# Causal attention: a head's ten transpositions in one row, the third chunk through another PSUM bank

## The chip, the cores and the metric

The kernel runs on one core of a Trainium2 chip. The metric is the device time of one execution in microseconds (us). The core's engines run side by side, each through its own list of instructions in order: TensorE (PE in the rows, its weight loads PEld), VectorE (DVE), ScalarE (ACT), GpSimd (POOL), and SyncE (SP), which issues most transfers. They wait for each other through semaphores. TensorE writes to PSUM, which has eight banks of 128x512 fp32 here; DVE and ACT read it.

## The reference

Two transformer layers on x of shape (4, 512, 512), fp32. The change lies in the attention of the first layer: 32 query heads and 8 key and value heads of width 128, causal, with rotary position codes.

```
q = (x @ wq).reshape(B, T, H, HD).transpose(0, 2, 1, 3)        # k and v alike, with 8 heads
q = q * cos + _rotate_half(q) * sin                             # k alike
scores = jnp.einsum('bhtd,bhsd->bhts', q, k) * (1.0 / np.sqrt(HD))
scores = jnp.where(mask, scores, -jnp.inf)
att = jax.nn.softmax(scores, axis=-1)
out = jnp.einsum('bhts,bhsd->bhtd', att, v)
return out.transpose(0, 2, 1, 3).reshape(B, T, H * HD) @ wo
```

The rest of the reference (layer norms with modulation, a sign-weight layer, a second attention over the heads of each position, a layer of routed low-rank experts) lies in other stages, which the change does not touch.

## The kernel before

The batch is worked in two halves of two items. In each half the attention of the first layer is one stage, `stage_groups`, which goes through 64 heads (32 query heads times two items). Every product is made of three products in a faster format: each operand is split into a high part, rounded by a cast on ACT (or DVE), and a low part, the difference, formed on DVE (or POOL). So a 128x512 result of one projection takes 4 x 3 = 12 products on TensorE.

The engines' lists are written out by hand in one loop over n, the head. At step n TensorE does the following (`block.tensor`, from line 788): it waits until head n's probabilities are normalised, transposes them (`turn`, line 698), projects a key or a value where one is due, forms the scores of head n+1, projects the query of head n+2, and then works on the pair p = n // 2: at an odd n it weighs the values (`weigh_early`, `weigh_late`), at an even n it multiplies three of the four output tiles of the pair before with the output weights (`out_proj`; the fourth comes at the odd n). A key is due at n = 5, 9, 13, ..., 57 (and at the very start), a value at n = 2, 6, ..., 58; the later text calls the former key steps and the latter value steps. At n = 4, 8, 12, ... and at n = 3, 7, 11, ... neither is due.

A head's probabilities under the causal mask are ten 128x128 blocks. They are transposed in three chunks of 4, 3 and 3 blocks (`PT_CHUNK`). Chunk 0 goes to bank pT0, chunk 1 to pT1, chunk 2 to pT0 again. ACT casts each chunk into `pth` (`pt_his`, line 865), then DVE subtracts into `ptl` (`pt_los`, line 978). Before, chunks 0 and 1 stand at the start of the step. Chunk 2 stands after the scores of head n+1 at a key step, ahead of the query's projection, and after the query's projection at all others:

```
turn(n, ((0, (0,)), (1, (1,))))
for e in step_e(n, 1): project(e)          # key or value
if n + 1 < NH: scores(n + 1)
if key_step(n): turn(n, ((2, (2, 3)),))
for e in step_e(n, 0): project(e)          # query
if not key_step(n): turn(n, ((2, (2, 3)),))
```

ACT and DVE have chunk 2 at the matching places of their lists. A projection lies in bank pj, and the next one may not begin before the last has been taken out: ACT writes two rotated half copies (lines 843 and 844), DVE multiplies by the cosine (`leave`, line 945), POOL multiplies by the sine and adds (lines 1143 and 1146), DVE casts the query's high part (line 963), POOL forms the low part (line 1155). For a head's softmax, DVE takes the maxima while it copies out of PSUM (`maxes`, line 974), ACT exponentiates (line 860), DVE takes the reciprocal and scales four rows of blocks (`norms`, lines 994 and 998).

The output tiles of `out_proj` go into bank pW, the second of each four into bank pO; `weigh_early` writes pO too. DVE adds each tile to the sum in SBUF (`add`, line 1006). So the third tile of a pair waits in pW for the addition of the first. At an even step DVE's list ends with the cosine of the query, the split of chunk 2, at value steps the split of the value, the addition of the first tile, the query's cast, the additions of the second and the third tile. In the first half, from n = 56 on, `modulate` puts other products between the second and the third tile.

Of the kernel before, what the change touches and what calls it, by code (L numbers as in the profile page):

```python
# [14 lines left out]
F32 = mybir.dt.float32  # L15
# [487 lines left out]
def stage_groups(nc, held, a, wts, half):  # L503
# [4 lines left out]
    with Stage(nc, f"gqa{half}") as st:  # L508
# [19 lines left out]
        pT = [st.ps(f"pT{i}", [P, T]) for i in range(2)]  # L528
        pO, pW = st.ps("pO", [P, T]), st.ps("pW", [P, D])
        early, late = (p[:].rearrange("p (h t) -> p h t", h=2) for p in (pO, pS[2]))  # L530
        qkv_in, wo_in = st.sem("qkv_in"), st.sem("wo_in")
# [41 lines left out]
        def last_split(kinds, group):  # L573
            return max(n for n, s in enumerate(SPLIT_LIST) if s[0] in kinds and s[2] == group) + 1

        def key_step(n):

            return any(PROJ[e][0] == "K" for e in step_e(n, 1))

# [4 lines left out]
        with nc.Block() as block:  # L584
# [39 lines left out]
            def _(pe):  # L624
# [74 lines left out]
                def turn(n, jobs):  # L699
                    for k, js in jobs:  # L700
                        if k == 0 and later and n > LATER_AT + 1:
                            pe.wait_ge(chunk_left, n - LATER_AT - 1)
                        if 3 * n + k >= 2:

                            pe.wait_ge(pt_lo, (3 * n, 3 * n - 1, 3 * n + 1)[k])
                        if k == 1 and n % R0 == R0 - 1 and n + 1 < NH:
                            pe.wait_ge(v_lo, n // R0 + 2)
                        if k == 1 and n == 0:
                            pe.wait_ge(v_lo, 1)
                        for j in js:  # L710
                            for i in range(j, TT):
                                c = PT_OFF[j] - PT_CHUNK[k][0] + (i - j) * P
                                mm = pe.transpose(pT[k % 2][:, c:c + P],  # L713
                                                  prob[n % 2][:, P_OFF[i] + j * P:P_OFF[i] + (j + 1) * P], held.ident)
                        mm.then_inc(pt_full, 1)
# [12 lines left out]
                def weigh_early(p):  # L728

                    if p == 0:  # L730
                        pe.wait_ge(cosed, 2)
                    else:
                        pe.wait_ge(w_added, TT * (p - 1) + 2)
                    pe.wait_ge(v_lo, 2 * p // R0 + 1)
                    weigh(p, early, [(0, 0, 0, PT_OFF[0], 2 * P), (1, 1, P, PT_OFF[1], P)])
# [7 lines left out]
                def out_proj(d):  # L743
# [4 lines left out]
                    if i == 0:  # L748
                        pe.wait_ge(o_lo, 2 * pair + 2)
                        pe.wait_ge(w_lo, split_no("o", (2 * pair + 1) % R0, pair // (R0 * HB // 2)))  # L750
                    before = [f for f in range(max(0, d - TT), d) if wbank(f) is wbank(d)]
                    if before:
# [37 lines left out]
                for n in range(NH):  # L790
# [3 lines left out]
                    pe.wait_ge(normed, n + 1)  # L794
                    turn(n, ((0, (0,)), (1, (1,))))
                    for e in step_e(n, 1):
                        project(e)
                    if n + 1 < NH:
                        scores(n + 1)
                    if key_step(n):  # L800
                        turn(n, ((2, (2, 3)),))
                    for e in step_e(n, 0):
                        project(e)
                    if not key_step(n):
                        turn(n, ((2, (2, 3)),))
                    if n % R0 == 2 and n // R0 + 1 < UNITS:
# [23 lines left out]
            def _(act):  # L830
# [33 lines left out]
                def pt_his(n, ks):  # L864
                    for k in ks:
# [3 lines left out]
                        c, w = PT_CHUNK[k]  # L869
                        nc.scalar.copy(pth[:, n % 2, c:c + w], pT[k % 2][:, 0:w]).then_inc(pt_hi, 1)  # L870

# [29 lines left out]
                for n in range(NH):  # L901
                    if n == 0:
                        for e in STEP_PROJ[0]:
                            leave(e)
                    pt_his(n, (0, 1))
                    for e in step_e(n, 1):
# [3 lines left out]
                    if n == NH - 2:  # L910
                        act.wait_ge(rope_lo, len(ROPE))
                        act.dma_start(x[:, TT:2 * TT, :], a["x"][(half * HB + 1) * T:(half * HB + 2) * T, :].rearrange("(j p) d -> p j d", p=P)
                                      ).then_inc(x_back, 16)
                    if key_step(n):
                        pt_his(n, (2,))
                    for e in step_e(n, 0):
                        leave(e)
                    if not key_step(n):
                        pt_his(n, (2,))
                    if n % R0 == 2 and n // R0 + 1 < UNITS:  # L920
# [15 lines left out]
            def _(dve):  # L936
# [41 lines left out]
                def pt_los(n, ks):  # L978
                    for k in ks:
                        dve.wait_ge(pt_hi, 3 * n + k + 1)  # L980
                        c, w = PT_CHUNK[k]
                        nc.vector.tensor_tensor(ptl[:, n % 2, c:c + w], pT[k % 2][:, 0:w], pth[:, n % 2, c:c + w].bitcast(F32),  # L982
                                                ALU.subtract).then_inc(pt_lo, 1)
# [97 lines left out]
                for n in range(NH):  # L1081
                    if n == 0:
                        for e in STEP_PROJ[0]:
                            leave(e)
                    pt_los(n, (0, 1))
                    for e in step_e(n, 1):
# [9 lines left out]
                    if n == NH - 1:  # L1096
                        first_residual(2)
                    if key_step(n):
                        pt_los(n, (2,))
                    for e in step_e(n, 0):  # L1100
                        leave(e)
                    if not key_step(n):
                        pt_los(n, (2,))
                    if n == NH - 1:
# [956 lines left out]
```

## Time and profile before

| | us |
|---|---|
| median of 3 runs (lowest 2176.83, highest 2181.4) | 2180.11 |
| the profiled execution's own time | 2177.08 |
| its span, first to last instruction | 2175.1 |
| PE busy (11441 products) | 1987.6 |
| DVE busy | 1483.2 |
| ACT busy | 1067.9 |
| POOL busy | 1039.8 |

The mean granted clock of TensorE is 0.957 of full speed. Over the two long stretches of `stage_groups` (100 to 750 us and 1200 to 1850 us) it is 1.00, and there the rows repeat every four heads. A row's time is the start; two products of 512 columns start about 0.23 us apart though each is drawn 0.39 us long, since they are pipelined. So the intervals between starts tell TensorE's pace, and its busy share does not.

### The profile page before, as it was taken

To read this page: it belongs to the slowest core of one execution; us is meant where nothing else is said; L and a number is where in the kernel's file an instruction comes from. 1 tells how busy PE (TensorE), PEld (TensorE's weight loads), DVE (VectorE), ACT (ScalarE), POOL (GpSimd) and SP (SyncE) were. 2 spreads that over 40 slices of the span, in tenths; PEclk is the share of its full clock that TensorE was granted. 3 is DMA by queue.
4 is the path that set the end of the run, shared out by engine and by line. 5 is a ranking of instruction groups with operands and counts; after the bars stand their busy time and mean duration, and the time that the engine had idled before them with its cause. 6 is when DMAs were issued, how large, how long until landed. Compare 5 with 4: busy or idle time off the path is not lost. (4 is left out here: it accounts for less than half of the span.)

```text
span 2175.1 us, 33305 instructions
## 1 busy us (share of the span) xinstructions
PE 1987.6 (91%) x11441; PEld 1596.0 (73%) x11441; DVE 1483.2 (68%) x3679; ACT 1067.9 (49%) x2422; POOL 1039.8 (48%) x801
## 2 busy tenths in 40 slices
PE   4899999999999996897948999999999999978797
PEld 3788888888888774475527888888888888745664
DVE  4666676766767666966756767676676667779386
ACT  3555555555555552433235555555555555543232
POOL 3546564645646431544046555555555555417241
PEclk8999999999999997898969999999999999988899
DMA  5000101011010234146321101010110100041561
GB/s 171 20 30 20 30 20 30 20 30 49 20 30 20 78 107 139 64 101 129 85 95 41 30 12 38 20 30 20 30 49 8 42 20 1 30 141 39 116 123 39
DMA packets 132007, 115.30 MB, mean 53 GB/s; under 512 B 43201, under 2 KB 93441, under 8 KB 131841
## 3 DMA queue, kind: packets, MB, share of 16 engines
q1 hardware_dynamic: 124784, 105.51, 16.8%
q10 hardware_dynamic: 7056, 7.68, 1.2%
q8 instruction: 93, 1.52, 0.3%
q14 instruction: 74, 0.60, 0.1%
HBM read 92.15 MB, written 16.81 MB: 50 GB/s over the span
## 5 line engine op out<-in xcount | busy, mean ns | idle before, releaser
L860 ACT ACTIVATE gqa_prob<-gqa_prob,gqa_nmax 128x256 f32<-128x256 f32 (+3 forms) x512 | 284.2, 556 | 154.9 <-DVE gqa_nmax L974 146.6
L870 ACT CAST gqa_pth<-gqa_pT 128x384 fp32r<-128x384 f32 (+1 forms) x384 | 185.5, 519 | 205.3 <-PE gqa_pT L713 202.9
L974 DVE CUSTOM_DVE_ANT_0 gqa_prob<-gqa_pS,consts 128x256 f32<-128x256 f32 (+3 forms) x512 | 222.7, 486 | 58.9 <-PE gqa_pS L677 56.9
L1143 POOL TENSOR_TENSOR x<-x,consts 128x512 f32<-128x512 f32 x80 | 107.3, 1341 | 312.3 <-ACT x L844 312.3
L1143 POOL TENSOR_TENSOR y<-y,consts 128x512 f32<-128x512 f32 x80 | 107.3, 1342 | 303.1 <-ACT y L844 303.1
L982 DVE TENSOR_TENSOR gqa_ptl<-gqa_pT,gqa_pth 128x384 fp32r<-128x384 f32 (+1 forms) x384 | 217.2, 594 | 24.4 <-ACT gqa_pth L870 24.3
L713 PE MATMUL gqa_pT<-consts,gqa_prob 128*128 128x128 f32 x1280 | 183.8, 275 | 20.7 <-DVE gqa_ptl L982 19.2
L655 PE MATMUL gqa_pj<-first_hh,wqh 128*128 128x512 f32 x496 | 195.9, 395 | 0.0
L655 PE MATMUL gqa_pj<-first_hh,wql 128*128 128x512 f32 x496 | 194.7, 393 | 0.0
L655 PE MATMUL gqa_pj<-first_hl,wqh 128*128 128x512 f32 x496 | 194.1, 391 | 0.0
L713 PEld LDWEIGHTS gqa_pT<-consts,gqa_prob 128*128 128x128 f32 x1280 | 154.3, 141 | 48.8 <-DVE gqa_prob L998 15.1
L998 DVE TENSOR_SCALAR gqa_prob<-gqa_prob,gqa_rden 128x128 f32<-128x128 f32 (+3 forms) x512 | 186.4, 427 | 4.6
L758 PE MATMUL gqa_pW<-woh,gqa_oh 128*128 128x512 f32 x380 | 163.3, 430 | 9.7 <-DVE x L1006 5.3
L677 PE MATMUL gqa_pS<-gqa_kh,gqa_qh 128*128 128x256 f32 (+3 forms) x512 | 165.5, 334 | 0.0
L677 PE MATMUL gqa_pS<-gqa_kl,gqa_qh 128*128 128x256 f32 (+3 forms) x512 | 156.6, 324 | 0.0
L758 PE MATMUL gqa_pW<-wol,gqa_oh 128*128 128x512 f32 x380 | 151.0, 397 | 0.0
L758 PE MATMUL gqa_pW<-woh,gqa_ol 128*128 128x512 f32 x380 | 150.8, 397 | 0.0
L677 PE MATMUL gqa_pS<-gqa_kh,gqa_ql 128*128 128x256 f32 (+3 forms) x512 | 144.4, 323 | 1.3 <-POOL gqa_ql L1155 1.3
L655 PE MATMUL gqa_pj<-first_hh,wkvh 128*128 128x512 f32 x248 | 104.2, 420 | 22.3 <-PEq L83 22.3
L994 DVE RECIPROCAL gqa_rden<-gqa_den 128x4 f32<-128x4 f32 x128 | 22.8, 178 | 136.3 <-ACT gqa_prob L860 136.3
L877 ACT CAST gqa_oh<-gqa_pS 128x512 fp32r<-128x512 f32 x64 | 37.5, 586 | 147.3 <-PE gqa_pS L724 147.3
L655 PEld LDWEIGHTS gqa_pj<-first_hh,wqh 128*128 128x128 f32 x496 | 93.2, 188 | 20.6
(333 smaller groups left out, 5284.4 us busy)
## 6 DMA issues: line engine op xcount, KB each, us to landing
raw_o<-in_wo SPq DMA_DIRECT2D x16, 1024.0 KB, 5.2
raw_q<-in_wq SPq DMA_DIRECT2D x14, 1024.0 KB, 5.6
raw_q<-in_wmod SPq DMA_DIRECT2D x10, 1024.0 KB, 5.2
raw_kv<-in_wkv SPq DMA_DIRECT2D x14, 512.0 KB, 6.8
vp<-mid_hf SPq DMA_DIRECT2D x64, 64.0 KB, 1.8
kp<-mid_hf SPq DMA_DIRECT2D x16, 256.0 KB, 2.3
qp<-mid_hf SPq DMA_DIRECT2D x16, 256.0 KB, 2.5
tail_bd<-vp SPq DMA_DIRECT2D x64, 64.0 KB, 3.0
```

The lines of the kernel that those rows point to most:

```text
L655: mm = pe.matmul(bank[e][:], wp, hp[:, k, t], start=(n == 0), stop=(n == 3 * KT - 1))
L677: mm = pe.matmul(pS[s][:, c:c + wide], qp[r][:, t], kp[u % 2][:, 0:wide], start=(m == 0), stop=(m == 2))
L713: mm = pe.transpose(pT[k % 2][:, c:c + P], prob[n % 2][:, P_OFF[i] + j * P:P_OFF[i] + (j + 1) * P], held.ident)
L758: mm = pe.matmul(wbank(d)[:], op[pair % 2][:, h % 2, t], wp[:, h % R0, :], start=(m == 0), stop=(m == 5))
L860: ins = nc.scalar.activation(p, p, ACT.Exp, scale=-1.0, bias=nmax[r][:, i:i + 1], accum_out=den[r][:, i:i + 1])
L870: nc.scalar.copy(pth[:, n % 2, c:c + w], pT[k % 2][:, 0:w]).then_inc(pt_hi, 1)
L877: nc.scalar.copy(oh[p % 2][:, :, part * HALF_T:(part + 1) * HALF_T], (early, late)[part]).then_inc(o_hi, 1)
L974: nc.vector.tensor_tensor_reduce(prob[r][:, P_OFF[i]:P_OFF[i] + w], pS[s][:, c:c + w], held.mask[:, T - w:T], -1.0, LARGEST, ALU.add, ALU.min,
L982: nc.vector.tensor_tensor(ptl[:, n % 2, c:c + w], pT[k % 2][:, 0:w], pth[:, n % 2, c:c + w].bitcast(F32), ALU.subtract).then_inc(pt_lo, 1)
L994: nc.vector.reciprocal(rden[n % 2][:], den[n % 2][:]).then_inc(recip, 1)
L998: ins = nc.vector.tensor_scalar(p, p, rden[n % 2][:, i:i + 1], None, ALU.mult)
L1143: nc.gpsimd.tensor_tensor(rot[r % 2][:], rot[r % 2][:], held.sinT, ALU.mult).then_inc(sined, 1)
```

## The change

All three chunks of head n are now transposed in a row at the start of the step, on TensorE, ACT and DVE. Chunk 2 goes to bank pO in place of pT0. With that go new waits: chunk 2 waits until pO has been emptied, at an odd head by DVE's addition of the pair's second tile (`w_added`), at an even one by the split of the output (`o_lo`); the writers of pO, `weigh_early` and the second tile of `out_proj`, wait for chunk 2's split (`pt_lo`). Chunk 0 waits no longer for chunk 2 of the head before. `key_step` goes.

```
+        turned = (pT[0], pT[1], pO)
...
-                        if 3 * n + k >= 2:
-
-                            pe.wait_ge(pt_lo, (3 * n, 3 * n - 1, 3 * n + 1)[k])
+                        if k < 2 and n:
+                            pe.wait_ge(pt_lo, 3 * n - 2 + k)
+                        elif k == 2 and n < 2:
+                            pe.wait_ge(cosed, 2)
+                        elif k == 2 and n % 2:
+                            pe.wait_ge(w_added, TT * (n // 2 - 1) + 2)
+                        elif k == 2:
+                            pe.wait_ge(o_lo, n - 1)
...
-                                mm = pe.transpose(pT[k % 2][:, c:c + P],
+                                mm = pe.transpose(turned[k][:, c:c + P],
...
+                    pe.wait_ge(pt_lo, 3 * (2 * p + 2))
                     pe.wait_ge(v_lo, 2 * p // R0 + 1)
                     weigh(p, early, [(0, 0, 0, PT_OFF[0], 2 * P), (1, 1, P, PT_OFF[1], P)])
...
+                    if i == 1 and d < NTILES - TT:
+                        pe.wait_ge(pt_lo, 3 * (2 * pair + 3))
...
-                    turn(n, ((0, (0,)), (1, (1,))))
+                    turn(n, ((0, (0,)), (1, (1,)), (2, (2, 3))))
                     for e in step_e(n, 1):
                         project(e)
                     if n + 1 < NH:
                         scores(n + 1)
-                    if key_step(n):
-                        turn(n, ((2, (2, 3)),))
                     for e in step_e(n, 0):
                         project(e)
-                    if not key_step(n):
-                        turn(n, ((2, (2, 3)),))
...
-                    pt_his(n, (0, 1))
+                    pt_his(n, (0, 1, 2))
...
-                    pt_los(n, (0, 1))
+                    pt_los(n, (0, 1, 2))
```

ACT's and DVE's lists lose chunk 2 at its former two places as TensorE's does, and the casts and subtractions read `turned[k]`. Three places of the built programs show the moves. In the names, gqa0 is the first half's stage and a last digit tells which of two or three buffers it is.

TensorE at the start of key step n = 5, behind the third output tile, before:

```order
L758 MATMUL gqa0_pW<-wol0,gqa0_oh1 128x512
L758 MATMUL gqa0_pW<-woh0,gqa0_ol1 128x512
L713 MATMUL gqa0_pT0<-consts,gqa0_prob1 128x128 x4
L713 MATMUL gqa0_pT1<-consts,gqa0_prob1 128x128 x3
L655 MATMUL gqa0_pj<-first0_hh,wkvh0 128x512
L655 MATMUL gqa0_pj<-first0_hl,wkvh0 128x512
L655 MATMUL gqa0_pj<-first0_hh,wkvl0 128x512
```

and now:

```order
L763 MATMUL gqa0_pW<-wol0,gqa0_oh1 128x512
L763 MATMUL gqa0_pW<-woh0,gqa0_ol1 128x512
L715 MATMUL gqa0_pT0<-consts,gqa0_prob1 128x128 x4
L715 MATMUL gqa0_pT1<-consts,gqa0_prob1 128x128 x3
L715 MATMUL gqa0_pO<-consts,gqa0_prob1 128x128 x3
L652 MATMUL gqa0_pj<-first0_hh,wkvh0 128x512
L652 MATMUL gqa0_pj<-first0_hl,wkvh0 128x512
L652 MATMUL gqa0_pj<-first0_hh,wkvl0 128x512
```

The three transpositions of chunk 2 stand between chunk 1 and the key's projection, and write pO.

TensorE later in the same step, from the last scores (bank pS2) to the query's projection, before:

```order
L677 MATMUL gqa0_pS2<-gqa0_kh1,gqa0_qh0 128x512
L677 MATMUL gqa0_pS2<-gqa0_kl1,gqa0_qh0 128x512
L677 MATMUL gqa0_pS2<-gqa0_kh1,gqa0_ql0 128x512
L713 MATMUL gqa0_pT0<-consts,gqa0_prob1 128x128 x3
L655 MATMUL gqa0_pj<-first0_hh,wqh0 128x512
L655 MATMUL gqa0_pj<-first0_hl,wqh0 128x512
L655 MATMUL gqa0_pj<-first0_hh,wql0 128x512
```

and now:

```order
L674 MATMUL gqa0_pS2<-gqa0_kh1,gqa0_qh0 128x512
L674 MATMUL gqa0_pS2<-gqa0_kl1,gqa0_qh0 128x512
L674 MATMUL gqa0_pS2<-gqa0_kh1,gqa0_ql0 128x512
L652 MATMUL gqa0_pj<-first0_hh,wqh0 128x512
L652 MATMUL gqa0_pj<-first0_hl,wqh0 128x512
L652 MATMUL gqa0_pj<-first0_hh,wql0 128x512
```

Nothing stands any more between the last scores and the query's projection, which writes the bank that the key is taken out of.

DVE from the end of step n = 4 into step n = 5 (the last scaled row, the query's cosine from pj, splits into ptl, additions from pW and pO, the query's cast qh, the key's cosine), before:

```order
L998 TENSOR_SCALAR gqa0_prob1<-gqa0_prob1,gqa0_rden1 128x512
L945 SCALAR_TENSOR_TENSOR x<-gqa0_pj,consts 128x512
L982 TENSOR_TENSOR gqa0_ptl<-gqa0_pT0,gqa0_pth 128x384
L1006 TENSOR_TENSOR y<-gqa0_pW,y 128x512
L963 CAST gqa0_qh0<-x 128x512
L1006 TENSOR_TENSOR y<-gqa0_pO,y 128x512
L1006 TENSOR_TENSOR y<-gqa0_pW,y 128x512
L982 TENSOR_TENSOR gqa0_ptl<-gqa0_pT0,gqa0_pth 128x512
L982 TENSOR_TENSOR gqa0_ptl<-gqa0_pT1,gqa0_pth 128x384
L945 SCALAR_TENSOR_TENSOR x<-gqa0_pj,consts 128x512
```

and now:

```order
L995 TENSOR_SCALAR gqa0_prob1<-gqa0_prob1,gqa0_rden1 128x512
L942 SCALAR_TENSOR_TENSOR x<-gqa0_pj,consts 128x512
L1003 TENSOR_TENSOR y<-gqa0_pW,y 128x512
L960 CAST gqa0_qh0<-x 128x512
L1003 TENSOR_TENSOR y<-gqa0_pO,y 128x512
L1003 TENSOR_TENSOR y<-gqa0_pW,y 128x512
L979 TENSOR_TENSOR gqa0_ptl<-gqa0_pT0,gqa0_pth 128x512
L979 TENSOR_TENSOR gqa0_ptl<-gqa0_pT1,gqa0_pth 128x384
L979 TENSOR_TENSOR gqa0_ptl<-gqa0_pO,gqa0_pth 128x384
L942 SCALAR_TENSOR_TENSOR x<-gqa0_pj,consts 128x512
```

The third split has left its place ahead of the first addition from pW and follows the second split; the addition from pO, for which chunk 2 of the odd head now waits, still stands behind the query's cast.

## Rows read from the trace of the kernel before

**Rows 1.** Windows: stretch, length; PE, PEld, DVE, ACT, POOL busy (instructions); granted clock; DMA.

```profile
1200.00:1300.00 100.00, 99.60 (x523) 83.93 (x522) 69.03 (x181) 56.69 (x136) 53.93 (x42) 1.00 0.06 17
```

**Rows 2.** Waits of TensorE: us in total, times, longest us.

```profile
PE gqa_pT L713 <- DVE gqa_ptl L982: 19.2, 4, 6.7
...
PE gqa_pW L758 <- DVE x L1006: 5.3, 16, 2.2
...
PE gqa_pW L758 <- DVE y L1006: 2.6, 14, 0.2
```

**Rows 3.** Timeline, TensorE, key step n = 21 of the second half: start, duration (us).

```profile
1410.33 0.40 PE L677 MATMUL gqa_pS<-gqa_kh,gqa_ql 128*128 128x512 f32 x1
1410.56 0.49 PE L713 MATMUL gqa_pT<-consts,gqa_prob 128*128 128x128 f32 x3
1410.84 0.50 PE L655 MATMUL gqa_pj<-first_hh,wqh 128*128 128x512 f32 x1
1411.18 0.39 PE L655 MATMUL gqa_pj<-first_hl,wqh 128*128 128x512 f32 x1
```

**Rows 4.** Timeline, DVE, the same step: the key's cosine from pj.

```profile
1410.09 0.69 DVE L945 SCALAR_TENSOR_TENSOR y<-gqa_pj,consts 128x512 f32<-128x512 f32 x1 [2.54 <-ACT y L844]
```

**Rows 5.** Timeline, TensorE, from step n = 20 into step n = 21.

```profile
1403.24 0.39 PE L758 MATMUL gqa_pO<-woh,gqa_ol 128*128 128x512 f32 x1
1403.64 0.50 PE L758 MATMUL gqa_pW<-woh,gqa_oh 128*128 128x512 f32 x1
...
1405.14 0.93 PE L713 MATMUL gqa_pT<-consts,gqa_prob 128*128 128x128 f32 x7
1405.82 0.48 PE L655 MATMUL gqa_pj<-first_hh,wkvh 128*128 128x512 f32 x1
1406.14 0.40 PE L655 MATMUL gqa_pj<-first_hl,wkvh 128*128 128x512 f32 x1
```

**Rows 6.** Timeline, DVE, step n = 20.

```profile
1396.39 1.14 DVE L982 TENSOR_TENSOR gqa_ptl<-gqa_pT,gqa_pth 128x512 fp32r<-128x512 f32 x2
...
1400.64 1.27 DVE L998 TENSOR_SCALAR gqa_prob<-gqa_prob,gqa_rden 128x128 f32<-128x128 f32 x4
1401.84 0.69 DVE L945 SCALAR_TENSOR_TENSOR y<-gqa_pj,consts 128x512 f32<-128x512 f32 x1
1402.44 0.55 DVE L982 TENSOR_TENSOR gqa_ptl<-gqa_pT,gqa_pth 128x384 fp32r<-128x384 f32 x1
1402.90 0.68 DVE L1006 TENSOR_TENSOR x<-gqa_pW,x 128x512 f32<-128x512 f32 x1
1404.58 0.43 DVE L963 CAST gqa_qh<-y 128x512 fp32r<-128x512 f32 x1 [0.99 <-POOL y L1146]
1404.92 0.68 DVE L1006 TENSOR_TENSOR x<-gqa_pO,x 128x512 f32<-128x512 f32 x1
```

**Rows 7.** Timeline, ACT, step n = 20: the query's second half copy.

```profile
1401.21 0.59 ACT L844 ACTIVATE y<-gqa_pj 64x512 f32<-64x512 f32 x1
```

**Rows 8.** Timeline, POOL, step n = 20: the query's sine.

```profile
1401.88 1.30 POOL L1143 TENSOR_TENSOR y<-y,consts 128x512 f32<-128x512 f32 x1 [2.34 <-ACT y L844]
```

**Rows 9.** Timeline, TensorE, value step n = 18: last product into pO, next two.

```profile
1382.29 0.39 PE L758 MATMUL gqa_pO<-woh,gqa_ol 128*128 128x512 f32 x1
1382.87 0.50 PE L758 MATMUL gqa_pW<-woh,gqa_oh 128*128 128x512 f32 x1 [0.19 <-DVE x L1006]
```

**Rows 10.** Timeline, DVE, value step n = 18: third split, the value's split, first addition.

```profile
1381.07 0.55 DVE L982 TENSOR_TENSOR gqa_ptl<-gqa_pT,gqa_pth 128x384 fp32r<-128x384 f32 x1
1381.53 0.68 DVE L950 TENSOR_TENSOR gqa_vl<-gqa_pT,gqa_vh 128x512 fp32r<-128x512 f32 x1
1382.13 0.68 DVE L1006 TENSOR_TENSOR x<-gqa_pW,x 128x512 f32<-128x512 f32 x1
```

**Rows 11.** Timeline, DVE, key step n = 21: the four scaled rows.

```profile
1413.89 1.80 DVE L998 TENSOR_SCALAR gqa_prob<-gqa_prob,gqa_rden 128x128 f32<-128x128 f32 x4
```

**Rows 12.** Timeline, POOL, key step n = 21: the key's low part.

```profile
1413.34 1.28 POOL L1155 TENSOR_TENSOR gqa_kl<-y,gqa_kh 128x512 fp32r<-128x512 f32 x1 [0.54 <-DVE gqa_kh L963]
```

More of the change, by code:

```diff
@@ L574, in last_split @@
             return max(n for n, s in enumerate(SPLIT_LIST) if s[0] in kinds and s[2] == group) + 1
-        def key_step(n):
-            return any(PROJ[e][0] == "K" for e in step_e(n, 1))
         def step_e(n, slot):
@@ L869, in pt_his @@
                         c, w = PT_CHUNK[k]
-                        nc.scalar.copy(pth[:, n % 2, c:c + w], pT[k % 2][:, 0:w]).then_inc(pt_hi, 1)
+                        nc.scalar.copy(pth[:, n % 2, c:c + w], turned[k][:, 0:w]).then_inc(pt_hi, 1)
                 def output_hi(p, part):
@@ L913, in _ @@
                                       ).then_inc(x_back, 16)
-                    if key_step(n):
-                        pt_his(n, (2,))
                     for e in step_e(n, 0):
                         leave(e)
-                    if not key_step(n):
-                        pt_his(n, (2,))
                     if n % R0 == 2 and n // R0 + 1 < UNITS:
@@ L981, in pt_los @@
                         c, w = PT_CHUNK[k]
-                        nc.vector.tensor_tensor(ptl[:, n % 2, c:c + w], pT[k % 2][:, 0:w], pth[:, n % 2, c:c + w].bitcast(F32),
+                        nc.vector.tensor_tensor(ptl[:, n % 2, c:c + w], turned[k][:, 0:w], pth[:, n % 2, c:c + w].bitcast(F32),
                                                 ALU.subtract).then_inc(pt_lo, 1)
@@ L1097, in _ @@
                         first_residual(2)
-                    if key_step(n):
-                        pt_los(n, (2,))
                     for e in step_e(n, 0):
                         leave(e)
-                    if not key_step(n):
-                        pt_los(n, (2,))
                     if n == NH - 1:
```

## The prediction

> **What bounds the kernel now.** I read the stretches of the program first. In the attention stage TensorE is drawn busy for 99.60 us of 100, at a granted clock of 1.00, which is the higher of its two levels, 2.4 GHz, while the other engines stay under 70 [rows 1]. So the stage goes at TensorE's pace, and the change takes nothing from TensorE's work: the same ten transpositions, the same products. It can only move waits. The table of TensorE's waits came next: four waits for the split of a chunk, 19.2 us in all, and 30 (16 and 14) for the addition that empties pW [rows 2]. Of these 30 one is 2.2 us long, at the end of a half; the other 29 are the value steps of both halves. Then I read the timeline of four heads engine by engine, since busy shares hide what is at stake here. An interval between starts that is longer than the usual 0.23 us is a wait.
>
> The reader is to see three such places. At the key step the query's projection starts at 1410.84, directly after chunk 2, and the key's cosine on DVE, which empties its bank pj, ends at 1410.09 + 0.69 = 1410.78 [rows 3, 4]. At an even step without a value the third output tile starts 0.40 us after the product before it and the next 0.34 after that: 0.17 + 0.11 = 0.28 us lost, because DVE ends the addition from pW only at 1402.90 + 0.68 = 1403.58 [rows 5, 6]. TensorE answers 0.06 us later. At a value step the same wait is longer, 0.58 - 0.23 = 0.35 us and the 0.11 of the restart [rows 9].
>
> **A unit price.** Seven transpositions take from 1405.14 to 1405.82, and the product behind them has 0.32 us in place of 0.23 [rows 5]: 0.68 + 0.09 = 0.77 us, 0.11 each with the change of kind included. So three cost 0.33 us. The group of three at the key step costs 0.28 + 0.34 - 0.23 = 0.39 [rows 3], 0.05 of it being the wait for pj.
>
> **Key steps: +9.2 us.** Here the change removes chunk 2 from between the last scores and the query's projection. That projection needs pj, and pj is free when the key's projection has been copied by ACT and multiplied by DVE. This chain starts with the end of the key's projection and has nothing ahead of it to speed up: DVE stood idle for 2.54 us before the cosine [rows 4]. So counted from the key's projection, the query still starts where it starts now, 1410.84. Without the transpositions TensorE is ready at 1410.56 and stands still. The three transpositions have filled time in which it would have waited; ahead of the key's projection they fill none and cost their whole 0.33 us. Keys fall at 14 steps in each half: 28 x 0.33 = 9.2 us. Nothing is saved if the third split, 0.46 us of DVE time (1402.44 to 1402.90, rows 6), slides into the 2.54 us of idling, which it does. Bounds: 28 x 0.28 = 7.8 (the gap that opens between 1410.56 and 1410.84) and 28 x 0.39 = 10.9.
>
> **Chunk 2 of the odd head behind pO: +5.3 us.** At an odd head chunk 2 must wait for DVE's addition of the tile in pO, and in DVE's list that addition stands behind the query's cast, which waits for POOL [rows 6]. In the step before, the query's projection now comes 0.33 us later, since chunk 2 has moved ahead of it. ACT's second half copy ends with it, at 1401.21 + 0.59 + 0.33 = 1402.13 [rows 7]; POOL's sine starts 0.33 later than 1401.88 [rows 8], the cast at 1404.91, the addition from pO at 1404.92 + 0.33 = 1405.25, ending 1405.93 [rows 6]; TensorE could begin to load the first block at 1405.98. Weight loads run one interval ahead, so TensorE is ready for that one at the start of the seventh transposition, 1405.14 + 6 x 0.11 = 1405.80, because chunks 0 and 1 start where they did (next part). A wait of 0.19 us. What is queued behind it is the whole of TensorE's list: the key or the next scores. This happens at n = 5, 9, 13, ... where no value step goes before: 15 in the second half, 13 in the first, where `modulate` delays the start from n = 57 on: 28 x 0.19 = 5.3 us. After a value step the addition from pO ends early enough, by 0.3 us. No wait of this kind stands in the trace, so: nothing if the start of the addition does not follow the query, 28 x 0.33 = 9.2 if TensorE is held for the whole delay. I take 0.19, which the rows give directly.
>
> **Even steps without a value: 0.** The third split goes from directly ahead of the first addition to behind the second split [rows 6]. It looks as if the addition would come 0.46 us earlier. But on DVE the list from 1396.39 on is one chain: splits, maxima, ACT's exponentials, scaled rows, cosine, addition. The split only changes its place in it: the scaled rows start 0.46 later, at 1401.10, the cosine at 1402.30, the addition at 1402.90 as before. TensorE's wait stays. Bounds: -30 x 0.28 = -8.4 if the wait vanished; the other side is the third rival.
>
> **Value steps: -3.8 us.** Here the value's projection leaves DVE time for the split, so the chain does become shorter by 0.46, but the query comes 0.33 later, and with it cosine, value split and addition [rows 10]: 0.46 - 0.33 = 0.13 us of the 0.46 us wait, 29 x 0.13 = 3.8 us. Bounds: 0 (the value's split also needs ACT's cast of it) and -29 x 0.46 = -13.3.
>
> **The rest: -0.5 us.** At n = 3, 7, 11, ... two groups of transpositions become one with no wait near; 0.39 - 0.05 - 0.33 = 0.01 to 0.02 us saved, 32 times: 0.5 us. The four long waits at the first and last heads [rows 2] are ended by the same DVE work in another order, one split of 0.46 more or less ahead of what TensorE waits for: 0, bounds 4 x 0.46 = 1.8 either way. The new waits of `weigh_early` and of the second output tile have at least the query's twelve products, 12 x 0.23 = 2.8 us, between the transpositions and themselves, and ACT and DVE split in that time: nothing.
>
> **Sum.** 9.2 + 5.3 - 3.8 - 0.5 = +10.2 us. The profiled execution took 2177.08 us (span 2175.1), so 2187.3; the median of the runs lies 3.0 us above it, and the same shift there gives 2190.3. I predict 2190.
>
> **Rivals.** First, faster. The freed place ahead of the first addition pulls that addition forward at all even steps, and TensorE's waits there go: 29 x 0.46 + 30 x 0.28 = 21.7 us less, 2158. For it: the split stands directly ahead of the addition in both places [rows 6, 10]. Against it: the chain of the part on even steps, and the key steps, which lose in any case. It decides if the scaled rows do not move by the split's 0.46. Chance 0.06.
>
> Second, half as slow. The addition from pO comes in time after all, and only the key steps count: 9.2 - 3.8 - 0.5 = +4.9, 2185. For it: today the addition ends 0.2 us before the load would be issued [rows 5, 6]. It decides if POOL's start moves by less than 0.15. Chance 0.14.
>
> Third, much slower. The scaled rows on DVE and POOL's operations disturb each other: four rows took 1.80 us at the key step in place of 1.27 [rows 6, 11], and POOL's low part ran from 1413.34 to 1414.62 across their start [rows 12]. At n = 4, 8, ... the scaled rows end at 1401.84 and the sine begins at 1401.88 today [rows 6, 8]; after the change the rows end at 1402.30 and the sine would begin at 1402.21. If the last row is caught, it waits for the whole 1.30 us and the addition after it too: about 28 x 1.2 = 34 us more on top, 2224. Against it: the last row starts some 0.4 us before its end, at 1401.90, 0.3 before POOL. Chance 0.05. The Trainium skill, SBUF — State Buffer, section Who interferes with whom, has the rule: VectorE in a two-port mode and GpSimd share one port pair, "Whoever issues first gets the shared pair for the whole instruction", and the other is blocked. By that rule the last row, issued first, keeps the pair and POOL loses about 0.1 us; rows 11 and 12 agree with a blocking of whole instructions.
>
> Fourth, no change: the placements offset each other more closely than I reckon. It would take a wait of under 0.05 at pO and the value steps at a gain of 0.3. Chance 0.05; 2180.
>
> **How the numbers follow.** Forecast 0.70, rivals 0.06, 0.14, 0.05, 0.05. The forecast's own range goes from both unknown terms at their ends (pO 0 to 9.2, values 0 to -3.8 and the rest): 2183 to 2199 on the median. The second and fourth rival stretch the lower end to 2180; at the upper end 2200 leaves out the third. About 0.2% (4.4 us) is what a measurement can tell from no change. Faster by more: the first rival and a little, 0.07. Within: the fourth and half of the second, 0.12. Slower: 0.81.
>
> **What would show it.** Right: at key steps an interval of about 0.5 us between the last scores and the query's first product, with DVE's cosine named as what ended it; at n = 5, 9, ... a break of about 0.2 us ahead of the transpositions into pO, ended by the addition at the line of `add`; the third tile's wait at 0.28 us at n = 4, 8, ... and about 0.33 at value steps; the scaled rows at n = 4, 8, ... 0.46 later against the start of the step. A period of four heads 0.37 us longer in sum (0.33 + 0.19 - 0.13 - 0.02). Wrong: the third tile without a wait, the query following the scores at 0.23 us, or scaled rows of over 2 us at n = 4, 8, ....

## The result and the profile after

The changed kernel takes 2189.05 us (median of 6 runs, 2186.57 to 2194.62), the kernel before 2179.35 beside it (6 runs, 2176.83 to 2182.2). The ratio is 1.0046 with a 95% interval from 1.0032 to 1.006, so the change costs 9.7 us. The profiled execution spans 2186.7 us.

The window that was read first, columns as in [rows 1], shows nothing of this:

```profile
1200.00:1300.00 100.00, 99.63 (x517) 83.29 (x516) 70.21 (x185) 56.02 (x138) 50.78 (x40) 1.00 0.06 17
```

TensorE is as busy as before at the same clock, and still gets through fewer products: 517 where [rows 1] has 523. The Trainium skill, Perfetto Trace Analysis, section Identifying the Most-Contended Engine, warns of this: since products are pipelined, their busy share is a poor measure, and the share of the weight loads a better one. The trace agrees: the loads (second pair of numbers) fall from 83.93 to 83.29 us. One hundred microseconds are only two periods of four heads; from 1200 to 1800 us the products fall from 3122 to 3099 and the loads from 502.97 to 499.31 us, while the busy time of the products stays (597.62 and 597.69).

The period of four heads tells more. Taken from the trace is the time from a head's first transposition to the next head's, in the second half, as a median over n = 4 to 52:

| | n = 4, 8, ... | key steps | value steps | n = 3, 7, ... | sum |
|---|---|---|---|---|---|
| before | 10.17 | 13.37 | 13.50 | 10.60 | 47.65 |
| after | 10.19 | 13.88 | 13.40 | 10.56 | 48.03 |
| predicted change | 0 | +0.52 | -0.13 | -0.02 | +0.37 |
| measured change | +0.02 | +0.51 | -0.10 | -0.04 | +0.38 |

(Each number is rounded by itself.)

Timeline of TensorE after (start, duration in us), the key step n = 21 of the second half; the last three rows answer to [rows 3], the first three to the end of [rows 5]:

```profile
1411.22 0.93 PE L715 MATMUL gqa_pT<-consts,gqa_prob 128*128 128x128 f32 x7
1412.09 0.55 PE L715 MATMUL gqa_pO<-consts,gqa_prob 128*128 128x128 f32 x3
1412.39 0.48 PE L652 MATMUL gqa_pj<-first_hh,wkvh 128*128 128x512 f32 x1
...
1416.90 0.40 PE L674 MATMUL gqa_pS<-gqa_kh,gqa_ql 128*128 128x512 f32 x1
1417.41 0.49 PE L652 MATMUL gqa_pj<-first_hh,wqh 128*128 128x512 f32 x1
1417.75 0.39 PE L652 MATMUL gqa_pj<-first_hl,wqh 128*128 128x512 f32 x1
```

The query's first product follows the last scores after 0.51 us in place of 0.23. Ahead of the transpositions into pO stand 0.87 us, where seven transpositions need 7 x 0.109 = 0.76: a break of 0.11, and the three take 0.30 where 0.25 is their pace (e2 below): 0.16 in all. Such a break stands at 28 of the heads n = 5, 9, ..., 13 in the first half and 15 in the second, as forecast. DVE's timeline over the same steps shows who ends both waits:

```profile
1407.17 1.28 DVE L995 TENSOR_SCALAR gqa_prob<-gqa_prob,gqa_rden 128x128 f32<-128x128 f32 x4
1408.36 0.68 DVE L942 SCALAR_TENSOR_TENSOR y<-gqa_pj,consts 128x512 f32<-128x512 f32 x1
1408.96 0.68 DVE L1003 TENSOR_TENSOR x<-gqa_pW,x 128x512 f32<-128x512 f32 x1
1411.01 0.43 DVE L960 CAST gqa_qh<-y 128x512 fp32r<-128x512 f32 x1 [1.37 <-POOL y L1139]
1411.35 0.68 DVE L1003 TENSOR_TENSOR x<-gqa_pO,x 128x512 f32<-128x512 f32 x1
...
1416.67 0.69 DVE L942 SCALAR_TENSOR_TENSOR y<-gqa_pj,consts 128x512 f32<-128x512 f32 x1 [2.51 <-ACT y L845]
```

The addition from pO ends at 1411.35 + 0.68 = 1412.03, 0.06 ahead of the transpositions into pO. The key's cosine ends at 1416.67 + 0.69 = 1417.36, 0.05 ahead of the query. The scaled rows begin 6.15 us after the head's first transposition at 1401.02 (second half, n = 20), where before they began 1400.64 - 1394.97 = 5.67 after it [rows 6]: 0.48 later. Cosine and first addition follow as before, and so the third tile still waits. TensorE's timeline at n = 20, and at the value step n = 18, answering to [rows 5, 9]:

```profile
1409.26 0.39 PE L763 MATMUL gqa_pO<-woh,gqa_ol 128*128 128x512 f32 x1
1409.69 0.50 PE L763 MATMUL gqa_pW<-woh,gqa_oh 128*128 128x512 f32 x1
1410.04 0.40 PE L763 MATMUL gqa_pW<-wol,gqa_oh 128*128 128x512 f32 x1
```

```profile
1388.55 0.39 PE L763 MATMUL gqa_pO<-woh,gqa_ol 128*128 128x512 f32 x1
1388.96 0.50 PE L763 MATMUL gqa_pW<-woh,gqa_oh 128*128 128x512 f32 x1
1389.30 0.40 PE L763 MATMUL gqa_pW<-wol,gqa_oh 128*128 128x512 f32 x1
```

An interval of 0.43 at n = 20 (0.40 before) and of 0.41 at the value step (0.58 before). The table of TensorE's waits, answering to [rows 2], no longer lists the value steps (28 of the 30 waits of [rows 2]; the other two, of 2.2 and 0.5 us at the last heads, stay); it does not list the breaks of the key steps either, so that a reader of this table alone would take the kernel for faster. What ends the long waits at the ends of the halves has changed:

```profile
PE gqa_pT L715 <- DVE gqa_prob L995: 13.7, 4, 6.5
...
PE gqa_pO L726 <- DVE gqa_ptl L979: 6.9, 2, 3.9
...
PE gqa_pW L763 <- DVE y L1003: 3.5, 1, 3.5
```

13.7 + 6.9 = 20.6 us stand where 19.2 + 0.6 = 19.8 stood: two of the four waits in the 13.7 are the first transpositions of each half, 0.3 us each, for which the table before has a row apart:

```profile
PE gqa_pT L713 <- DVE gqa_prob L998: 0.6, 2, 0.3
```

The 6.9 us are waits of `weigh_early` for chunk 2's split at the last head of each half. The 3.5 us belong to step n = 62 of the first half; before, a wait of 4.4 us stood in that step at a product of `modulate`.

### The profile page after: what moved, and what is told of

It reads as the page before. It is cut to its first block and busy times, and to the rows that moved or that the text cites. A ratio compares the mean times of both kernels' runs of the same rounds, so it can differ in the third digit from the quotient of the medians.

```text
span 2186.7 us, 33429 instructions
## 1 busy us (share of the span) xinstructions
PE 1998.0 (91%) x11441; PEld 1597.9 (73%) x11441; DVE 1505.4 (69%) x3679; ACT 1069.0 (49%) x2422; POOL 1035.8 (47%) x801
## 5 line engine op out<-in xcount | busy, mean ns | idle before, releaser
L871 ACT CAST gqa_pth<-gqa_pT 128x512 fp32r<-128x512 f32 (+1 forms) x256 | 124.7, 541 | 195.4 <-PE gqa_pT L715 195.2
L995 DVE TENSOR_SCALAR gqa_prob<-gqa_prob,gqa_rden 128x128 f32<-128x128 f32 (+3 forms) x512 | 215.7, 484 | 4.5
L979 DVE TENSOR_TENSOR gqa_ptl<-gqa_pT,gqa_pth 128x512 fp32r<-128x512 f32 (+1 forms) x256 | 146.9, 615 | 18.0 <-ACT gqa_pth L871 18.0
L674 PE MATMUL gqa_pS<-gqa_kl,gqa_qh 128*128 128x256 f32 (+3 forms) x512 | 157.1, 325 | 0.0
L715 PE MATMUL gqa_pT<-consts,gqa_prob 128*128 128x128 f32 x896 | 121.2, 276 | 14.6 <-DVE gqa_prob L995 13.7
L715 PEld LDWEIGHTS gqa_pT<-consts,gqa_prob 128*128 128x128 f32 x896 | 104.9, 142 | 26.1 <-DVE gqa_prob L995 15.4
```

What stands on the lines that cost most here:

```text
L674: mm = pe.matmul(pS[s][:, c:c + wide], qp[r][:, t], kp[u % 2][:, 0:wide], start=(m == 0), stop=(m == 2))
L715: mm = pe.transpose(turned[k][:, c:c + P], prob[n % 2][:, P_OFF[i] + j * P:P_OFF[i] + (j + 1) * P], held.ident)
L871: nc.scalar.copy(pth[:, n % 2, c:c + w], turned[k][:, 0:w]).then_inc(pt_hi, 1)
L979: nc.vector.tensor_tensor(ptl[:, n % 2, c:c + w], turned[k][:, 0:w], pth[:, n % 2, c:c + w].bitcast(F32), ALU.subtract).then_inc(pt_lo, 1)
L995: ins = nc.vector.tensor_scalar(p, p, rden[n % 2][:, i:i + 1], None, ALU.mult)
```

## The experiments

Theory A is the prediction's account: four separate waits, each at its own bank (pj at key steps, pO at odd heads, pW at both kinds of even steps), each with the price given there. The rivals hold that DVE's list is the one thing behind them, so that a wait which is taken away comes back at the next bank. In most of the runs one wait is given back or taken away, and the step that holds it is read.

**e1: the key steps back.** At key steps chunk 2 goes back to its old place and to pT0 (the same on ACT and DVE); all other heads stay in a row.

```
+        def in_row(n):
+            return not key_step(n)
+        def turned(n, k):
+            return pT[k] if k < 2 else pO if in_row(n) else pT[0]
...
-                    turn(n, ((0, (0,)), (1, (1,)), (2, (2, 3))))
+                    turn(n, ((0, (0,)), (1, (1,)), (2, (2, 3)))[:2 + in_row(n)])
...
+                    if key_step(n) and not in_row(n):
+                        turn(n, ((2, (2, 3)),))
```

> The changed kernel, but at the 28 key steps chunk 2 goes back between the last scores and the query's projection, into pT0, with its split at the old place; all other heads keep the ten transpositions in a row. Theory A (the loss sits at the key steps: the transpositions paid ahead of the key, and the wait for pO in front of them): a key step gets 0.33 + 0.16 us shorter, 28 x 0.49 = 13.7 us, so about 2175, some 4 us below the kernel before. Rival B (the third split ahead of the maxima delays every head's softmax a little, so the loss is spread over all heads): 28 of 128 heads get back 0.08 us each, 2187.

Measured: 2174.33 us, ratio 0.9971 [0.996, 0.9982] to the kernel before. The key step is at 13.38 again, the other three are at 10.17, 13.40 and 10.56. So the whole loss sits at the key steps, rival B is out, and without them the change would gain.

**e2: pO emptied first.** At even steps DVE adds the tile in pO ahead of the query's cast instead of behind it.

```
+                    if p and n % 2 == 0:
+                        add(TT * (p - 1) + 1)
                     for e in step_e(n, 0) if n else STEP_PROJ[0][1:]:
                         rope_parts(e)
...
-                    elif p:
-                        add(TT * (p - 1) + 1)
```

> The changed kernel, but at even steps DVE adds the tile in pO ahead of the query's cast, which waits for POOL. Theory A: chunk 2 of the next head then finds pO empty, the break of 0.11 + 0.05 us ahead of it goes at 28 steps, -4.6 us, 2184.5; the key steps keep the interval of 0.5 us between scores and query. Rival C (the break only moves: the cast comes later and the query's parts miss the next scores): 2189.

Measured: 2182.29 us, ratio 1.0016 [1.0007, 1.0024]. TensorE and DVE at n = 20 and 21:

```profile
1404.63 0.93 PE L730 MATMUL gqa_pT<-consts,gqa_prob 128*128 128x128 f32 x7
1405.39 0.49 PE L730 MATMUL gqa_pO<-consts,gqa_prob 128*128 128x128 f32 x3
1405.64 0.48 PE L663 MATMUL gqa_pj<-first_hh,wkvh 128*128 128x512 f32 x1
```

```profile
1403.12 0.69 DVE L1027 TENSOR_TENSOR x<-gqa_pO,x 128x512 f32<-128x512 f32 x1
1404.44 0.43 DVE L984 CAST gqa_qh<-y 128x512 fp32r<-128x512 f32 x1 [0.63 <-POOL y L1167]
```

The break is gone: 0.76 us for seven transpositions, 0.25 for three. The key step falls from 13.88 to 13.70, so the wait at pO cost 0.18 and 28 of them 5.0 us. The 0.33 that stay above 13.37 are the wait at pj. The medians differ by 6.8 us, more than the 4.6 expected. The other steps became a little shorter too (n = 4, 8, ... by 0.02, the value steps by 0.01), so that four heads take 47.83 in place of 48.03: 0.21 in each of some 31 periods is 6.5 us.

**e3: the value steps back.** As e1, with the heads n = 2, 6, ... at the old place.

```
         def in_row(n):
-            return not key_step(n)
+            return n % R0 != 2
```

> The changed kernel, but at the value steps (n = 2, 6, 10, ...) chunk 2 goes back behind the query's projection, into pT0, with its split at the old place. Theory A: only the gain of these steps is lost, 29 x 0.13 = 3.8 us, so slower, 2193. Rival B (the split ahead of the maxima costs each head): a quarter of the heads gets its loss back, 2186.5.

Measured: 2191.96 us, ratio 1.0062 [1.0048, 1.0076]. The value step is 13.50 again, the others stay, and the waits of the value steps are back in the table. 29 x 0.10 = 2.9 us. The medians differ by as much, but the intervals of the two ratios (1.0032 to 1.006 for the changed kernel) overlap, so the steps decide and not the medians. The value steps are where the change gains.

**e4: the first tile first, without the change.** The kernel before, with the first tile's addition drawn ahead of the third split at all even steps.

```
+                    if n % 2 == 0 and n // 2:
+                        add(TT * (n // 2 - 1))
                     if not key_step(n):
                         pt_los(n, (2,))
...
-                    if p:
-                        add(TT * (p - 1) + 3 * (n % 2))
+                    if p and n % 2:
+                        add(TT * (p - 1) + 3)
```

> The kernel before, but at even steps DVE adds the first output tile directly behind the query's cosine, ahead of the split of chunk 2 and of the value's split. Theory A (at even steps TensorE waits for DVE's list alone, whose end the change only reorders): the waits of the third tile go, 29 x 0.46 + 30 x 0.28 = 21.7 us less than the kernel before, 2158. Rival D (the next thing on DVE is late in its place: the split that chunk 0 of the next head waits for in pT0): half of it or less, 2169 to 2180.

Measured: 2157.96 us, ratio 0.9903 [0.989, 0.9917]. TensorE and DVE at n = 20:

```profile
1391.49 0.39 PE L758 MATMUL gqa_pO<-woh,gqa_ol 128*128 128x512 f32 x1
1391.72 0.39 PE L758 MATMUL gqa_pW<-woh,gqa_oh 128*128 128x512 f32 x1
```

```profile
1390.09 0.69 DVE L945 SCALAR_TENSOR_TENSOR y<-gqa_pj,consts 128x512 f32<-128x512 f32 x1
1390.69 0.68 DVE L1006 TENSOR_TENSOR x<-gqa_pW,x 128x512 f32<-128x512 f32 x1
1391.29 0.55 DVE L982 TENSOR_TENSOR gqa_ptl<-gqa_pT,gqa_pth 128x384 fp32r<-128x384 f32 x1
```

The third tile follows after 0.23 us. This is the 2158 of the first rival, reached by another way: the split that stood ahead of the addition did cost 21 us, but the change puts it ahead of the maxima, where at even steps without a value it delays the addition just as much. Only behind the addition is it out of the way.

**e5: the gap filled.** In the changed kernel the fourth output tile, six products that nothing holds up, goes into the gap of the key steps.

```
                     if n + 1 < NH:
                         scores(n + 1)
+                    if key_step(n):
+                        out_proj(TT * (n // 2 - 1) + 3)
...
                         weigh_early(p)
-                        if p:
+                        if p and not key_step(n):
                             out_proj(TT * (p - 1) + 3)
```

> At key steps the fourth output tile of the pair (twelve... its products into pW) is issued between the last scores and the query's projection instead of behind the early products of PV. Everything else is as in the changed kernel. Theory A (the 0.51 us between the last scores and the query's first product is TensorE waiting for the bank pj with nothing to do): the tile fills it, 28 x (0.51 - 0.23 + 0.11) = 28 x 0.39 = 10.9 us less than the changed kernel's 2189, 2178; the step of a key goes from 13.88 to about 13.49. Rival: the third split's new place delays DVE's whole list by the same amount, so that the wait only moves to the next product that needs DVE: 2187 to 2191.

Measured: 2177.27 us, ratio 0.9989 [0.9978, 1.0]. TensorE at n = 21:

```profile
1410.21 0.40 PE L678 MATMUL gqa_pS<-gqa_kh,gqa_ql 128*128 128x512 f32 x1
1410.45 0.39 PE L767 MATMUL gqa_pW<-woh,gqa_oh 128*128 128x512 f32 x1
...
1411.60 0.39 PE L767 MATMUL gqa_pW<-woh,gqa_ol 128*128 128x512 f32 x1
1411.83 0.39 PE L656 MATMUL gqa_pj<-first_hh,wqh 128*128 128x512 f32 x1
```

Every interval is 0.23 or 0.24, and the step takes 13.51 in place of 13.88. The other steps keep 10.17, 13.40 and 10.56, so the wait does not come back elsewhere and the rival is out. The gap at pj was time without work, which chunk 2 had filled before.

**e6: all waits at once.** e5, and DVE's additions in the order in which TensorE needs the banks: the first tile ahead of the query's cosine (at value steps ahead of the value's split), the tile in pO ahead of the query's cast.

```
+                    if n % 4 == 0 and n:
+                        add(TT * (n // 2 - 1))
                     for e in step_e(n, 0):
                         leave(e)
...
+                    if n % 4 == 2 and n // 2:
+                        add(TT * (n // 2 - 1))
                     if n % R0 == 2 and n // R0 + 1 < UNITS:
                         value_los(n // R0 + 1)
...
-                    if p:
-                        add(TT * (p - 1) + 3 * (n % 2))
+                    if p and n % 2:
+                        add(TT * (p - 1) + 3)
+                    elif p:
+                        add(TT * (p - 1) + 1)
```

> The changed kernel with the tile moved into the gap of the key steps as in the run before, and with DVE's additions ordered by when TensorE needs the bank: the first tile's addition ahead of the query's cosine at even steps without a value and ahead of the value's split at value steps, the second tile's (in pO) ahead of the query's cast. Theory A (each of the waits at pj, pO and pW is a wait of its own, and TensorE has work in all of them): 10.9 less at the key steps, 28 x 0.18 to 0.24 = 5 to 7 less at pO, 29 x 0.30 and 30 x 0.31 = 18 less at the third tile: 2189 - 35 = 2154 (2150 to 2158), at or below the 2158 of the kernel before with the first tile's addition drawn forward; a period of four heads of 46.7 or less in place of 48.03. Rival (the waits share one cause, DVE's list, and drawing one addition forward pushes the query's cosine back and with it the query's projection's successors): 2160 to 2170.

Measured: 2153.18 us, ratio 0.9881 [0.9868, 0.9895], the lowest median of all. Steps 9.83, 13.31, 13.08 and 10.53, sum 46.75. The window from 1200 to 1300 us:

```profile
1200.00:1300.00 100.00, 100.00 (x531) 85.99 (x529) 69.99 (x186) 57.15 (x140) 55.80 (x44) 1.00 0.09 27
```

TensorE is drawn without a gap there, and the weight loads are at 85.99 us. Intervals between starts that are longer than the usual one for their size still add 0.4 us per four heads (1.6 in the changed kernel), nearly all of them behind transpositions. The gains add up: 35.9 us against the changed kernel, 35 expected. So the waits are separate ones; those at pW were taken away by themselves only in the kernel before (e4). Against e4, which needs neither the row nor the bank, the period is 0.18 shorter; the intervals of the two ratios overlap a little (0.989 to 0.9895), so the times alone do not set the two apart.

**e7 and e8: each half of the change alone.** e7 is the kernel before with chunk 2 in pO, at its old place in all lists. e8 has all ten transpositions in a row and split in a row, but chunk 2 in pT0, behind chunk 0 of the same head. Both use the helper of e1. In e7 the two calls that place chunk 2 stay as they stand in the kernel before, in e8 they are gone; the places in the lists of ACT and DVE follow that of TensorE.

```
         def in_row(n):                       # e7: chunk 2 in pO
+            return True
...
-                    turn(n, ((0, (0,)), (1, (1,)), (2, (2, 3)))[:2 + in_row(n)])
+                    turn(n, ((0, (0,)), (1, (1,)), (2, (2, 3)))[:2])
```

```
         def in_row(n):                       # e8: chunk 2 in pT0
+            return False
...
-                    turn(n, ((0, (0,)), (1, (1,)), (2, (2, 3)))[:2 + in_row(n)])
+                    turn(n, ((0, (0,)), (1, (1,)), (2, (2, 3))))
```

> The kernel before with one half of the change alone: the third chunk goes into PV's bank pO, but stays at its old place in all lists, behind the scores and the projections, so that its split stands late in the lists of ACT and DVE. Theory A (the bank pays only with the early split, since the early products of PV and the second output tile then stand directly behind the chunk and wait for both of its halves): at the 62 odd steps about 2.4 us each and at the 60 even ones about 0.9, 150 to 200 us more than before, 2330 to 2380. Rival (the bank costs nothing by itself, the place of the split costs what was measured): 2175 to 2190.

> The other half of the change alone: all ten transpositions in a row on TensorE, split in a row on ACT and DVE, but the third chunk still into pT0, where it has to wait until ACT and DVE have split the first chunk of the same head. Theory A: the third chunk's transpositions wait for that split, ACT's copy (about 0.6 us) and DVE's (0.55) after the first chunk is full, less the 0.33 us of the second chunk: 1.3 us at each of 126 heads, 150 to 170 us more, 2330 to 2360. Rival (the bank does not matter, the splits are in time): 2185 to 2195, as the changed kernel.

Measured: e7 2409.55 us, ratio 1.1059 [1.1039, 1.1079]; e8 2354.06 us, ratio 1.0804 [1.0785, 1.0824]. TensorE's waits in e7, then TensorE and DVE in its key step n = 21:

```profile
PE gqa_pO L743 <- issue: 137.3, 60, 2.4
PE gqa_pO L781 <- DVE gqa_ptl L1005: 43.3, 62, 6.7
```

```profile
1569.02 0.39 PE L663 MATMUL gqa_pj<-first_hh,wql 128*128 128x512 f32 x1
1571.78 0.47 PE L743 MATMUL gqa_pO<-gqa_pth,gqa_vh 128*128 128x512 f32 x1 [2.38 <-issue]
```

```profile
1569.43 1.79 DVE L1021 TENSOR_SCALAR gqa_prob<-gqa_prob,gqa_rden 128x128 f32<-128x128 f32 x4
1571.13 0.55 DVE L1005 TENSOR_TENSOR gqa_ptl<-gqa_pO,gqa_pth 128x384 fp32r<-128x384 f32 x1
```

The table names nothing for the first wait, but DVE's split of pO ends at 1571.68, 0.10 ahead of the product that may then overwrite the bank. The odd steps lose 2.69 and 2.45 us, as expected of theory A; the even ones 0.75 and 0.17, less than the 0.9 expected. Four heads lose 6.06 by these medians, and the halves from first to last head 114 and 111 us where 63 / 4 x 6.06 = 95 would follow. The whole is 230 us, above the 150 to 200 expected. Most of the 34 us beyond the medians goes with the clock: in about ten odd steps of each half the granted clock falls, and such a step takes some 1.5 us longer than its like. TensorE in one of them, n = 17 of the second half (17.50 us at a mean granted clock of 0.90; the kernel before has 1.00 over that stretch):

```profile
1516.64 0.77 PE L743 MATMUL gqa_pO<-gqa_pth,gqa_vh 128*128 128x512 f32 x1 [2.39 <-issue]
1517.20 0.63 PE L743 MATMUL gqa_pO<-gqa_ptl,gqa_vh 128*128 128x512 f32 x1
1517.63 0.63 PE L743 MATMUL gqa_pO<-gqa_pth,gqa_vl 128*128 128x512 f32 x1
```

After the wait of 2.39 us the products start 0.43 us apart in place of 0.23; from 1516.64 to 1519.55 the granted clock is 0.50, the lower of its two levels (1.2 GHz). So some 30 of the 230 us are not waiting but the lower clock, which none of the other kernels shows in this stretch. e8 by the same views:

```profile
PE gqa_pT L730 <- DVE gqa_ptl L1003: 157.1, 128, 3.4
```

```profile
1520.34 0.93 PE L730 MATMUL gqa_pT<-consts,gqa_prob 128*128 128x128 f32 x7
1522.54 0.55 PE L730 MATMUL gqa_pT<-consts,gqa_prob 128*128 128x128 f32 x3 [1.27 <-DVE gqa_ptl L1003]
```

All 128 heads wait, 157.1 / 128 = 1.23 us each; the granted clock from 1500 to 1600 us is 1.00 (0.97 in e7). The row needs the other bank and the bank needs the early split: each alone costs 8 to 11%, both together 0.5%.

## Why the prediction was right, point by point

**Key steps, +9.2 us.** Right. The interval of 0.51 was forecast at about 0.5, ended by the cosine; it stands at all 28 key steps. 0.33 per step is what is left at the key step when e2 takes the other wait away. e5 shows the reason given: the transpositions had filled time in which TensorE would have waited.

**Behind pO, +5.3 us.** Right in place, count and cause; the size was 0.19 (its own times, 1405.98 - 1405.80, give 0.18) and is 0.18 by e2, 0.16 by the intervals of one step. The addition's end was forecast 0.79 us after the head's first transposition (1405.93 - 1405.14) and came 0.81 after it (1412.03 - 1411.22). POOL's sine starts 0.32 later against the start of its step (1408.25 - 1401.02 = 7.23 in place of 1401.88 - 1394.97 = 6.91), 0.33 by the forecast. Rival two, without this wait, is out.

**Even steps without a value, 0.** Right. The scaled rows came 0.48 later (0.46 forecast), and the wait became no shorter: 0.43 in place of 0.40, +0.02 us per step. This also removes the first rival. (The interval of 0.40 stands at 28 steps, not 30: in the first half `modulate` stands ahead of the third tile at n = 56 and 60. The rival's price of 21.7 is 21.2 by that count.)

**Value steps, -3.8 us.** Right in sign and place. Measured -0.10 per step, 2.9 us by e3. The wait's interval itself shrank by 0.17, from 0.58 to 0.41, more than the 0.13 forecast. The moved transpositions do not take the rest: chunks 0 to 2 cost 0.68 + 0.33 us before and 1.01 in a row. What shows are pieces of 0.02 us or less in the intervals of the output tiles, which stay unexplained. The prediction took the 29 from the table of waits, where 28 of the 30 are value steps; by the intervals of the timeline there are 29, since the one at n = 2 of the second half is too short for the table.

**The rest, -0.5 us.** The steps n = 3, 7, ... gained 0.04 each in place of 0.015, 1.3 us. The long waits at the first and last heads grew by 0.8 us, within the 1.8 allowed; among them is a wait of `weigh_early` at the last head, where no query's products stand in between and which the forecast had put at nothing. The one at n = 62 shrank by 0.9; the forecast had not counted it. The pieces add up to 9.2 + 5.0 + 0.6 - 2.9 - 1.3 + 0.8 - 0.9 = 10.5 us, where 10.2 were forecast and 9.7 measured, with an interval of 7.0 to 13.1. That the small terms missed in both directions and nearly cancel is luck; the two large ones, and with them the sign, are not.

The two traces differ by more, 2186.7 - 2175.1 = 11.6 us. In the changed kernel's trace step n = 1 takes 12.0 and 12.1 us in the two halves, at a mean granted clock of 0.75, where 10.7 and 11.1 stood at 0.86 and 0.82. e2, whose list has the same row and bank, takes 10.9 and 11.1 there, so most of these 2.4 us cannot be put down to the change.

**Rival three, at another place.** At n = 4, 8, ... the scaled rows keep 1.28 us and POOL's sine beside them becomes only 0.05 longer than in [rows 8]:

```profile
1408.25 1.35 POOL L1136 TENSOR_TENSOR y<-y,consts 128x512 f32<-128x512 f32 x1 [2.28 <-ACT y L845]
```

The blocking that it feared occurs at the key steps, where the prediction did not reckon with it. DVE and POOL, and the two last scaled rows by themselves (shortest, median, longest in ns):

```profile
1420.47 2.88 DVE L995 TENSOR_SCALAR gqa_prob<-gqa_prob,gqa_rden 128x128 f32<-128x128 f32 x4
```

```profile
1421.77 1.30 POOL L1136 TENSOR_TENSOR y<-y,consts 128x512 f32<-128x512 f32 x1 [0.56 <-ACT y L845]
```

```profile
L995 DVE TENSOR_SCALAR gqa_prob<-gqa_prob,gqa_rden x2: 407/977/1547, 1421.5 to 1421.8; 128x384 f32<-128x384 f32 x1, 128x512 f32<-128x512 f32 x1
```

The rows begin 0.50 us later than before against the start of the step, and POOL's sine starts just before the last one: four rows take 2.88 us where 1.80 stood [rows 11], the last alone 1.55. The rule of the Trainium skill that the prediction weighed (SBUF — State Buffer, Who interferes with whom: the one that issues first holds the shared ports for its whole instruction) agrees here in who loses, 1.07 us by DVE at key steps and 0.05 by POOL at n = 20. It agrees in size only for DVE, whose row ends 0.28 us after POOL's product: at n = 20 POOL's sine starts 0.2 us before the end of DVE's last row (1407.17 + 1.28 = 1408.45 above) and loses 0.05, not 0.2. The blocking costs nothing in the end: the rows end at 1423.35 and TensorE needs them for head 22 at 1425.10. e5 bears this out: its rows are back at 1.81 us in the median, and its step gained 0.37, which is the gap alone (0.39). So the third rival's price was real and its place was not on the path.

## What to carry to other kernels

Work that is moved out of a wait which it filled costs its whole length, though nothing was added (0.33 us at each key step here); so before moving a piece, look for what the engine would do in its place, and fill the gap with work that waits for nothing (e5). An operation that is drawn forward in one engine's list shortens a wait only if it leaves the chain that ends the wait: ahead of the maxima the split delayed the addition as before, behind the addition it gave 21 us (e4). Waits at separate banks are counted one by one, and e6 shows that the gains then add here. A wait can cost more than its length: in e7 the granted clock fell behind some of the waits of 2.4 us, while it stays at 1.00 in e8 with waits of 1.2 us and in the kernels with waits of 0.1 to 0.3 us.

## What was not expected of the hardware

One DVE row of 128x512 took 1.55 us when POOL's product had started 0.03 us ahead of it, 0.48 us without, and POOL's product 1.30 us there. In e7 the granted clock fell to 0.50 behind a wait of 2.4 us in about ten odd steps of each half, and not in the others. TensorE began 0.05 to 0.06 us after DVE's last write to the bank it waited for (1412.03 to 1412.09, 1417.36 to 1417.41), as the prediction had it, but 0.10 after it in e7 (1571.68 to 1571.78).
